# Attention and a mixture of experts on one core: the work before the first sequence spread over the first sequences

## The reference

```python
xn = layernorm(X)                                   # over 128, no scale
Q, K, V = xn @ Wq + bq, xn @ Wk, xn @ Wv            # 16 heads of 64
R = xn @ Wr + br                                    # 16 heads of 10
extra = einsum('bhtn,ntp->bhtp', R, D_ntT)          # b_nd by distance, 128 wide, causal
W = softmax(Q @ K.T / 8 + bias + extra)             # bias: -1e9 outside 0 <= t - p < 128
attn = (W @ V) @ Wproj + bproj
logits = xn @ router_w.T                            # 8 experts
top2 values, indices -> weights by softmax
moe = sum over the 2 of weight * (gelu(xn @ w1[e].T + b1[e]) @ w2[e].T + b2[e])
out = X + attn + moe
```

## Time and profile before

| | |
|---|---|
| three runs | 1452.96, 1454.41, 1458.62 us; median 1454.41 |
| the profiled execution, its own time | 1453.4 us |
| its span, first to last instruction | 1451.6 us |
| granted TensorE clock, mean | 0.964 of full speed |
| busy: PE, DVE, ACT, POOL | 1330.1, 910.6, 935.4, 769.1 us |
| PE over the span | 92% |
| DMA | 298.86 MB, 206 GB/s |

### The profile page before, as it was taken

How to read it: one execution, slowest core, us unless ns; L and a number is a source line. 1 busy time by engine, 2 the same in 40 slices (tenths; PEclk the granted TensorE clock), 3 DMA queues, 4 the chain that set the end, 5 groups by cost and what they waited for, 6 DMA issues and landing times.

```text
span 1451.6 us, 35450 instructions
## 1 busy us (share of the span) xinstructions
PE 1330.1 (92%) x10631; PEld 1116.0 (77%) x10631; DVE 910.6 (63%) x3651; ACT 935.4 (64%) x2960; POOL 769.1 (53%) x1518
## 2 busy tenths in 40 slices
PE   2482899999999999987999999999999999999996
PEld 1131688888888888876999999888788888888885
DVE  4577577777777777762112112278787877877886
ACT  1121677777777777764444444487777777777774
POOL 1241576777776777760000000077777777777765
PEclk8695899999999999998999999999999999999999
DMA  9774777677777667766666666467677767777773
GB/s 292 263 271 152 200 220 219 200 213 213 201 214 223 204 197 204 217 184 201 207 206 198 207 206 198 132 187 201 189 215 213 221 194 222 200 213 221 213 218 86
DMA packets 458699, 298.86 MB, mean 206 GB/s; under 512 B 20586, under 2 KB 432788, under 8 KB 458516
## 3 DMA queue, kind: packets, MB, share of 16 engines
q1 hardware_dynamic: 450324, 279.86, 65.4%
q0 software_dynamic: 8192, 16.79, 3.7%
HBM read 135.01 MB, written 145.77 MB: 193 GB/s over the span
## 4 chain that ended last, share of the span: by engine, by line
PE 62%; DMA 15%; SPq 10%; issue 5%; DVE 4%; POOL 3%; ACT 1%; DVEq 0%; another core or an unknown queue 0%; POOLq 0%; ACTq 0%
DMA skew<-gst 12%; PE ps L1346 10%; PE ps L1423 8%; PE ps L1442 8%; PE ps L1310 7%; PE ps L1312 7%; PE ps L1311 7%; PE ps L1410 5%; PE ps L1452 5%; PE ps L1379 4%; SPq L491 4%; SPq L472 1%; SPq L463 1%; PE ps L1328 1%; SPq L390 1%
## 5 line engine op out<-in xcount | busy, mean ns | idle before, releaser
L810 ACT ACTIVATE prob<-logit,low 128x128 f32<-128x128 f32 x1024 | 402.0, 396 | 31.5 <-DVE low L1113 16.4
L692 POOL TENSOR_SCALAR prob<-prob,inv 128x128 f32<-128x128 f32 x512 | 188.3, 368 | 387.9 <-DVE inv L1129 377.4
L1113 DVE CUSTOM_DVE_ANT_0 logit<-ps,extra 128x128 f32<-128x128 f32 x1024 | 255.8, 287 | 112.4 <-PE ps L1423 80.5
L1423 PEld LDWEIGHTS ps<-qk 64*128 64x128 f32 x2048 | 166.3, 187 | 58.6 <-issue 47.2
L1095 DVE TENSOR_TENSOR probT<-ps,keep 128x512 f32<-128x512 f32 x256 | 175.7, 686 | 52.8 <-PE ps L1410 43.4
L1423 PE MATMUL ps<-qk 64*128 64x256 f32 (+1 forms) x2048 | 202.1, 337 | 0.0
L1442 PE MATMUL ps<-probT,val 128*64 128x256 f32 (+1 forms) x2048 | 194.7, 332 | 5.2 <-DVE acc L1159 4.2
L810 ACT ACTIVATION_READ_ACCUMULATOR prob<-logit,low 128x1 f32 x1024 | 195.0, 190 | 0.0
L694 POOL TENSOR_SCALAR prob<-prob,inv 128x128 f32<-128x128 f32 x512 | 186.9, 365 | 0.0
L800 ACT COPY qk<-ps 128x512 f32<-128x512 f32 x256 | 150.6, 588 | 34.6 <-PE ps L1312 17.6
L1442 PEld LDWEIGHTS ps<-probT,val 128*64 128x64 f32 x2048 | 128.1, 136 | 57.0 <-DVE probT L1097 3.2
(11 more groups left out here) (177 smaller groups left out, 2508.8 us busy)
## 6 DMA issues: line engine op xcount, KB each, us to landing
skew<-gst SPq DMA_DIRECT2D x384, 256.0 KB
extra<-skew SPq DMA_DIRECT2D x256, 256.0 KB, 3.4
...
rT<-r_hi SPq DMA_DIRECT2D x128, 80.0 KB
...
```

The source lines that it names most:

```text
L692: nc.gpsimd.tensor_scalar(prob[:, h, 0:P], prob[:, h, 0:P], inv[:, h, 0:1], 1.0, ALU.mult, ALU.mult).then_inc(norm_made, 1)
L810: ins = nc.scalar.activation(prob[:, h % PB, cols], logit[:, h % LB, cols], ACT.Exp, scale=-1.0, bias=low[:, h % LB, t:t + 1], accum_out=t ...
L1113: ins = nc.vector.tensor_tensor_reduce(out=logit[:, h % LB, cols], in0=ps[:, b + n, cols], in1=extra[:, h, cols], scale=1.0, scalar=BIG, o ...
L1423: mm = nc.tensor.matmul(ps[:, S_BANK[pair % 2][n], cols], qk[rows, pair % 2, 0, q], qk[rows, pair % 2, 1, k], start=True, stop=True)
```

## The change

**Loads and constants.** SP loads the small tensors first, then X in quarters with `Wr`, `Wq`, `Wk` and `Wv` between them; `bproj` and `Wproj` come later. Biases are one row each, and PE adds them into the column sums by a product with minus one.

**Layer norm.** The statistics are turned into deviations in two parts (16 tiles, then 48). POOL normalises 12 of the 16 blocks, DVE blocks 6, 9, 12 and 15 (`XN_DVE`). PE makes the router's logits rows of 128 straight into one PSUM bank, and DVE copies them once. PE interleaves blocks 4 to 15 with the first units of sequence 0. `xn_d` is gone.

**Work moved into the sequences.** The routing is cut into 17 pieces, one at DVE's end of each of slots 0 to 16 (`routing`). PE adds the counts as a unit in slot 9. PE turns one of the 16 matrices of `w1` and `w2` in each of sequences 0 to 16 but the third, as a unit in slot 1; ACT copies it, and SP loads and stores it. `bproj` is added by POOL, one block in each of slots 0 to 15. `x_place` is zeroed only at its last seven blocks (slots 2 to 8) and behind each expert's last row (`zero_pads`, eight DMAs in slot 14, their rows read from SBUF).

**Rows.** X is loaded again for them, two tiles at a time into one of four buffers, three slots ahead, and DVE normalises them there (`norm_rows`). The 128 spreading calls are spaced evenly over slots 18 to 76, and the 128 fetching calls over slots 81 to 125, slot 0 of a sequence included; `at_now` is gone. `add_rows` comes block by block, four instructions in one slot for each choice.

**Experts.** They run at the start of sequence 20. `w1` comes as it is, and POOL splits it (`split_weights`), three instructions for each place.

```diff
-    HALF = B // 2
+    SURE = TOP * B * T // BANK
+    HALF = B // 2 + 4
+    XR = 4
...
+        COUNT_AT = 2
+        TURN_AT = [i for i in range(2 * NX + 1) if i != COUNT_AT]
+        ALL, UNIT_AT, TURN_UNIT = list(START), {}, []
+        for i in range(B):
+            for d, place_at, kind, k, t, ahead in UNITS:
+                if ahead and i + 1 == B:
+                    continue
+                UNIT_AT.setdefault((4 * i + d, place_at), []).append(len(ALL))
+                ALL.append((kind, k, t, i + ahead))
+                if (d, place_at) == (1, 1):
+                    if i == COUNT_AT:
+                        UNIT_AT[4 * i + d, 2] = [len(ALL)]
+                        ALL.append(("c", 0, 0, i))
+                    elif i in TURN_AT:
+                        UNIT_AT[4 * i + d, 3] = [len(ALL)]
+                        TURN_UNIT.append(len(ALL))
+                        ALL.append(("w", TURN_AT.index(i), 0, i))
+        DS = 4 * B
+        SPREAD_FROM, SPREAD_DS = 18, 4 * (HALF - 1) + 1 - 18
+        FETCH_FROM, FETCH_DS = 4 * HALF + 1, DS - 2 - (4 * HALF + 1)
+        spread_at = [SPREAD_FROM + m * SPREAD_DS // (TILES * TOP) for m in range(TILES * TOP)]
+        fetch_at = [FETCH_FROM + m * FETCH_DS // (TILES * TOP) for m in range(TILES * TOP)]
+        rows_at = [spread_at[4 * j] for j in range(TILES // 2)]
+        block_at = [fetch_at[8 * n + 7] for n in range(BLOCKS)]
+        def add_at(n, later):
+            return max(block_at[n] + 1 + later, QUADS * (2 * n + 2) + 1)
...
+            def zero_pads():
+                sp.wait_ge(owner_made, 1)
+                for e in range(NX):
+                    row = sp.value_load(pad_row[0:1, e:e + 1], min_val=0, max_val=PLACES * BANK)
+                    sp.dma_start(x_place[bass.ds(row, BANK), :].rearrange("(p r) e -> p r e", r=PER), zeros).then_inc(zeroed, 16)
+            def fetch_rows(j):
+                wait_from(sp, spread[j % XR], j // XR * 64)
+                sp.dma_start(xrow[:, j % XR, :, :], x_v[:, 2 * j:2 * j + 2, :]).then_inc(xrow_in[j % XR], 16)
...
+            pool.wait_ge(rstd_ready, 1)
+            for k in range(4):
+                norm_block(k)
+            pool.wait_ge(xnT_made, 1)
+            split_q(0, 0)
+            round_weights(0)
+            pool.wait_ge(rstd_ready, 2)
+            for k in (4, 5, 7, 8, 10):
+                norm_block(k)
+            pool.wait_ge(wv_centred, 2)
+            nc.gpsimd.tensor_scalar(wv_hi[:, :], wv_r[:, :], 1.0, 1.0, ALU.mult, ALU.mult).then_inc(wv_split, 1)
+            for k in (11, 13, 14):
+                norm_block(k)
+            pool.wait_ge(wv_split, 1)
+            nc.gpsimd.tensor_tensor(wv_lo[:, :], wv_r[:, :], wv_hi[:, :].bitcast(F32), ALU.subtract).then_inc(wv_split, 1)
...
+            def fetch_row(m):
+                n, t, k = m // (PER * TOP), m // TOP % PER, m % TOP
+                if m == 0:
+                    pool.wait_ge(y_out[0], (PLACES + 1) // 2 * 16)
+                    pool.wait_ge(y_out[1], PLACES // 2 * 16)
+                if m % (PER * TOP) == 0:
+                    wait_from(pool, added, 2 * TOP * (n - 1))
+                nc.gpsimd.indirect_dma_start(yget[:, n % 2, t, k, :], None, table_y,
+                                             bass.IndirectOffsetOnAxis(place[:, PER * n + t, k:k + 1], 0)
+                                             ).then_inc(fetched[n % 2], 16)
...
+            def split_weights(b, u):
+                pool.wait_ge(w1raw_in[u], 16 * (b // 2 + 1))
+                wait_from(pool, hid_made, (b - 1) * FC)
+                nc.gpsimd.tensor_copy(b1b[:, u, :], w1raw[:, u, FF:RAW1])
+                nc.gpsimd.tensor_copy(w1b[:, u, 0:FF], w1raw[:, u, 0:FF]).then_inc(w1_high, 1)
+                pool.wait_ge(w1_high, b + 1)
+                nc.gpsimd.tensor_tensor(w1b[:, u, FF:2 * FF], w1raw[:, u, 0:FF], w1b[:, u, 0:FF].bitcast(F32),
+                                        ALU.subtract).then_inc(w1_low, 1)
...
+            dve.wait_ge(rstd_ready, 2)
+            for k in XN_DVE:
+                dve.wait_ge(xnT_psum, k - 1)
+                for n in range(PER):
+                    ins = nc.vector.tensor_scalar(xn[:, k % 2, n, :], acc[:, PER * k + n, :],
+                                                  mean[:, PER * k + n:PER * k + n + 1],
+                                                  rstd[:, PER * k + n:PER * k + n + 1], ALU.subtract, ALU.mult)
+                ins.then_inc(xn_dve, 1)
+            dve.wait_ge(lg_psum, BLOCKS)
+            nc.vector.tensor_copy(lg[:, :, :], ps[:, LG_BANK, :].rearrange("p (t e) -> p t e", e=NX)).then_inc(lg_made, 1)
...
+                elif q == 5:
+                    link(nc.vector.tensor_tensor(one2[:, :, :], one2[:, :, :], over(r1), ALU.is_equal))
+                    nc.vector.tensor_tensor(m2[:, :], m2[:, :], m1[:, :], ALU.subtract).then_inc(route, 1)
+                    link(nc.vector.tensor_tensor(chosen[:, :, :], one1[:, :, :], one2[:, :, :], ALU.add))
+                elif q == 6:
+                    sums(scan[0], chosen, 1, TILES)
+                    sums(scan[1], scan[0], 2, TILES)
...
+            def norm_rows(j):
+                dve.wait_ge(xrow_in[j % XR], (j // XR + 1) * 16)
+                for t in range(2):
+                    n = 2 * j + t
+                    ins = nc.vector.tensor_scalar(xrow[:, j % XR, t, :], xrow[:, j % XR, t, :], mean[:, n:n + 1],
+                                                  rstd[:, n:n + 1], ALU.subtract, ALU.mult)
+                ins.then_inc(xrow_made, 1)
...
                     if heads:
+                        routing(q)
+                        for j, at_q in enumerate(rows_at):
+                            if at_q - 1 == q:
+                                norm_rows(j)
+                        for n in range(BLOCKS):
+                            for later in range(TOP):
+                                if add_at(n, later) == q:
+                                    add_rows(n, 2 * later)
+                                    add_rows(n, 2 * later + 1)
...
-            def router(k):
-                pe.wait_ge(xnT_made, k + 1)
-                wait_from(pe, lgT_made, k)
-                nc.tensor.matmul(ps[0:NX, LGT_BANK, :], rwT[:, :], xnT[:, at(k * BANK, BANK)],
-                                 start=True, stop=True).then_inc(lgT_psum, 1)
+            def router(k):
+                pe.wait_ge(xnT_made, k + 1)
+                for n in range(PER * k, PER * k + PER):
+                    mm = nc.tensor.matmul(ps[:, LG_BANK, n * NX:(n + 1) * NX], xnT[:, n * P:(n + 1) * P], rwT[:, :],
+                                          start=True, stop=True)
+                mm.then_inc(lg_psum, 1)
...
+                elif kind == "w":
+                    pe.wait_ge(w_in[n % 2], (n // 2 + 1) * 16)
+                    for c in range(FC):
+                        mm = nc.tensor.transpose(ps[:, MISC_BANK, c * P:(c + 1) * P], w_raw[:, n % 2, c * P:(c + 1) * P],
+                                                 ident[:, :])
+                elif kind == "c":
+                    pe.wait_ge(tally_made, 1)
+                    nc.tensor.matmul(ps[:, MISC_BANK, 0:NX], lower[:, :], tally[:, :], start=True, stop=True)
+                    mm = nc.tensor.matmul(ps[:, MISC_BANK, NX:2 * NX], ones[:, :], tally[:, :], start=True, stop=True)
...
+            pe.wait_ge(wr_split, 2)
+            unit(0)
+            pe.wait_ge(wq_in, 32)
+            pe.wait_ge(small_made, 4)
+            for k in range(2):
+                column_sums(Q_MEAN_BANK[k], wqk_r[:, 0, k * BANK:(k + 1) * BANK], bq_row[:, k * BANK:(k + 1) * BANK])
+            pe.wait_ge(wk_in, 16)
+            for k in range(2):
+                column_sums(K_MEAN_BANK[k], wqk_r[:, 1, k * BANK:(k + 1) * BANK], None)
+            pe.wait_ge(wv_in, 16)
+            pe.wait_ge(qk_centred, 2)
+            for k in range(2):
+                column_sums(V_MEAN_BANK[k], wv_r[:, k * BANK:(k + 1) * BANK], None)
+            pe.wait_ge(basis_in, 3 * PER * 16)
+            for k in range(4, BLOCKS):
+                turn(k)
+                if k > 4:
+                    router(k - 1)
+                if k - 3 < len(START):
+                    unit_taken(pe, k - 4)
+                    unit(k - 3)
+            router(BLOCKS - 1)
+            pe.wait_ge(qk_low, 2)
+            pe.wait_ge(wv_split, 2)
+            keys(0, 0)
+            keys(0, 1)
+            pe.wait_ge(wv_centred, 2)
+            pe.wait_ge(lg_made, 1)
+            for i in range(B):
+                if i == HALF:
```

1104 lines of the change are left out of this document (513 added, 591 removed).

## The result

| | before | forecast | after |
|---|---|---|---|
| median of the runs, us | 1456.5 | | 1436.8 |
| ratio, 95% interval | | 0.959 | 0.9866, 0.9822 to 0.9910 |
| profiled execution's own time, us | 1453.4 | 1394 | 1432.05 |
| first keys | 146.3 | 64 (56 to 75) | 88.5 |
| sequence 0 | 53.1 | 53.1 | 54.6 |

A forecast was written before the change was run, and what follows sets the result against it. The prediction took the time as 146 us of preparation, 32 sequences that PE fills, and the experts. From 1453.4 us, -82 + 7 + 8 + 3 + 4 - 6 + 9 - 2 = -59 gave 1394, range 1370 to 1424.

The forecast's parts named there:

- Twelve blocks are left: Start, blocks 4 to 15: two buffers, POOL 1.46 us a block; block 6 ready at 50, block 15 at 61.6, keys at 64.
- POOL normalises blocks 0 to 3: Start, first blocks: 16 POOL norm instructions at 0.365 us end at 21.7, leading to sequence 0's R at about 27.
- The longest hold: Start: DVE waits for PE's column sums of Wq until 33, so the second half's deviations come at 42 us.
- Turning weights: Turning sequences: 16 times four transposes on PE at 0.44 us add 7 us; bounds 0 and 7.
- DMA and SP: Turning sequences: extra transfers and three more SP issues a sequence cost 0.25 us in each of 16, +4; bounds 0 and 18.
- The rival on SP: Turning sequences: SP falls behind, positions come 5.15 us late in each of 16, 82 us for 4, total 1472; chance 0.04.
- Padding: Slot 14: SP's chain of eight loads and issues takes 8.8 us, of which 3 were counted; bounds 0 and 9.
- Routing: Sequences: 25.3 us of DVE work in 17 slots, ahead of the inverses, costs 0.5 a slot, +8; bounds 0 and 25.
- Adding `bproj`: Sequences: 1.29 us a slot on POOL, in slots without spreading, costs 0.
- The late load: Before the experts: POOL's 5.15 us wait for `xrow` goes with four buffers three slots ahead, -6; bounds -6 and 0.
- lock: Rival: POOL and DVE block each other, 34 us lost in `norm_rows` and routing, half covered, total 1411; chance 0.06.
- longer start: Rival: the two buffers or SP's queue put the first keys at 84 us, total 1414; chance 0.08.

The follow-up runs named there:

- e2: Changed kernel with DVE normalising blocks 6 to 15 and POOL's list of later blocks cut to 4 and 5; 0.990 of the time before the change.
- e4: Changed kernel with DVE normalising blocks 6 to 15 and three of four router products left out; 0.973 of the time before the change.
- e1: Changed kernel with DVE's last 16 statistics and second deviations moved ahead of its wait for PE's column sums; 0.979 of the time before the change.
- n1: Changed kernel with POOL's norms using one per-row operand, the mean's subtraction left out; 0.978 of the time before the change.
- t3: Changed kernel without weight turning: no transposes, ACT copies, or turning loads and stores; 0.968 of the time before the change.
- t2: Changed kernel without the turned matrices' loads and stores, PE's transposes and ACT's copies kept; 0.968 of the time before the change.
- a0_again: The changed kernel run once more, unaltered; 0.988 of the time before the change.

## Why the prediction was wrong

The direction held, the size did not: -59 was forecast, -21.4 came, 38 us too few, outside the range.

- **"Twelve blocks are left ... POOL (8 blocks, 1.46 each) and DVE take turns with PE" failed, and it is most of the 24 us.** It gave PE's side of the loop no time, though the change puts 1.7 us of router and 1.1 of turn there, 2.5 a block as they overlap, at the lower level. And it took 0.365 for POOL's norm from an instruction with one per-row operand, and the one used has two: 0.78. Twelve blocks took 34.9 us from 53.5 for the 14 from 50 to 64. e2 to e4 show PE's pace as the bound and POOL's right behind it: 0.9 for POOL alone, 6.8 for PE alone, 17.9 for both.
- **"POOL normalises blocks 0 to 3 ... 21.7" failed by the same row:** 27.3. R came at 31.5 for 27, since PE's routers of blocks 2 and 3, again at no cost in the sum, stood ahead of it. The column sums took 7.9 us for 6.6 and ended at 40.7 for 33. The row of 6.63 us was read as wholly at the lower level, but before the clock rose within it (0.50 up to 40 us, 0.71 from 40 to 42). The deviations were ready at 48.5 for 42. "The longest hold" was the right place and kind: DVE waited 19.99 us there. e1 gave 9.2 us for the hold, and n1 9.0 for POOL's operands, half of it through the hold.
- **"Turning weights: 7" and "DMA and SP: +4" failed.** Sequences 0 to 16 took 19 us less in t3's profile than in the changed kernel's, for the 11, and 17 of them in sequences 5 to 15. PE's part was the smaller one and not the larger: t2 less t3 give 0.1 a sequence, the transfers 1.1 to 1.4. The rival on SP had the sign of this, late transfers, at 5.15 us a sequence: over three times too much. (By the sum that rival decides from 4.4 us a sequence, not 4.6.)
- **Padding** cost 4.3 us in sequence 3, for 3; with the padding in that sequence the profiles have 35.5 to 41.5 us, so it is good to some us only. **Routing** in t3's sequences 0, 1, 2 and 4, with no turning there but with the bias in it, comes to 5 us for 8. **Adding `bproj`**, 0, was about 1.4 in sequences 0 and 1.
- **The late load**, -6, the **experts**, 0 (the 2.1 at the change to them did not come again in a0_again, 311.9), **fetching**, 9.3 for 9 in this one execution, and norm_rows at a median of 340 ns, no lock, were right. The end gave nothing for the 2.
- The rival *longer start*, keys at 84, was the nearest and had 8 in 100. Its reason was buffers or SP; the true one was two engines' busy time. A sum over PE alone would have shown that 64 could not hold: from its first block at 18 us, 16 blocks of 2.5, 13 us of column sums and some 4 of R and units are an estimated 75. The router's new form had no row in the trace before, and needed a guess; it got nothing.
